# Attention v and q read from PSUM by VectorE, and the blocks of a step laid out anew, in a fused graph layer (gather, attention, routed FFN)

## The reference, cut to what matters

```python
xn = layernorm(x)                                        # 12500 nodes x 256
x  = x + gnn(xn) + mix(xn)[0]
x  = x + ffn(layernorm(x))                               # for the routed half of the nodes

def gnn(x):                                              # 212500 edges
    agg = segment_sum(edge_val[:, None] * x[src], dst)
    return relu(((1 + eps) * x + agg) @ W1.T + b1) @ W2.T + b2

def mix(x):                                              # one node is a sequence of length 1
    h = relu(batchnorm(conv(logmap(x), w_qkv)))          # 768 channels
    t = logmap(proj(expmap(h)))                          # a scale per row
    s = conv(conv(t, w_dw), w_pw)                        # both halves: 1536 channels
    q, k, v = split(scaled(concat(t, s)))                # 16 groups of 32 each
    q, k = relu(q), relu(k)
    out = (v k^T) q / (v + ATT_EPS)                      # = v * q * sum_group(k) / (v + eps)
    ft = logmap(expmap(out)) @ w_res.T + b_res
    return proj(expmap(ft))
```

## Time and profile before

| what | us |
|---|---|
| median of 3 runs | 2632.83 (2632.32 to 2636.76) |
| the profiled execution, its own time | 2637.63 |
| span of that execution | 2636.0 |
| PE busy in the span | 2489.5 (94%), 12654 matmuls |
| DVE busy | 1806.4 (69%) |
| ACT busy | 1464.7 (56%) |
| POOL busy | 1753.3 (67%) |

### The profile page before, as it was taken

The page is one execution under the profiler, slowest core; times in us unless marked ns, Lnnn a source line. Parts: engine busy times, 40 slices in busy tenths (PEclk is TensorE's granted clock), DMA queues, the critical chain, the costliest instruction groups (busy, mean ns, idle before and its releaser), DMA issues.

```text
span 2636.0 us, 42907 instructions
## 1 busy us (share of the span) xinstructions
PE 2489.5 (94%) x12654; PEld 2172.5 (82%) x12654; DVE 1806.4 (69%) x5986; ACT 1464.7 (56%) x3513; POOL 1753.3 (67%) x1858
## 2 busy tenths in 40 slices
PE   5688899999999999999999999999999999999997
PEld 4466688888888888888888888888788888888886
DVE  5754676767767677776776867667676776777657
ACT  4453555655556565565655556556565655656531
POOL 0006777777777777777777777777777777777600
PEclk9798999999999999999999999999999999999998
DMA  7433444344444444434344444443434444343338
GB/s 228 153 115 88 119 118 127 114 121 124 120 125 115 120 124 120 125 116 128 115 121 123 117 126 114 121 123 115 126 115 126 118 121 121 111 129 114 108 116 278
DMA packets 195537, 333.37 MB, mean 126 GB/s; under 512 B 47839, under 2 KB 138013, under 8 KB 195209
## 3 DMA queue, kind: packets, MB, share of 16 engines
q0 software_dynamic: 85216, 233.60, 31.1%
q1 hardware_dynamic: 105018, 92.42, 10.9%
q10 hardware_dynamic: 5072, 4.57, 0.6%
HBM read 291.99 MB, written 38.46 MB: 125 GB/s over the span
## 4 chain that ended last, share of the span: by engine, by line
PE 76%; DVE 9%; ACT 6%; DMA 6%; issue 2%; ACTq 1%; POOL 1%; SPq 0%; DVEq 0%; POOLq 0%
PE bank L1168 23%; PE qkv L1263 13%; PE bank L1275 12%; PE bank L1182 9%; PE bank L1212 6%; PE qkv L1192 4%; DMA work<-in_x 4%; PE qkv L1191 2%; PE bank L1228 2%; PE bank L1237 2%; PE bank L1202 2%; DVE rings L975 2%; DMA rings<-xn_dram,window 1%; DVE work L407 1%; ACT work L465 1%
## 5 line engine op out<-in xcount | busy, mean ns | idle before, releaser
L781 POOL DMA_INDIRECT rings<-xn_dram,window x1764 | 1740.5, 987 | 651.3 <-issue 381.4
L1168 PE MATMUL bank<-rings 128*128 128x256 f32 x3528 | 891.9, 381 | 28.1 <-DMA rings<-xn_dram,window 16.3
L1168 PEld LDWEIGHTS bank<-rings 128*128 128x128 f32 x3528 | 654.6, 190 | 130.2 <-DVE rings L975 32.8
L975 DVE TENSOR_SCALAR rings<-iota,window_dst,window 128x128 f32<-128x128 f32 x1764 | 559.8, 364 | 150.3 <-PE bank L1168 136.2
L1263 PE MATMUL qkv<-work,ffn_weights 128*128 128x256 f32 x1568 | 362.9, 380 | 0.0
L1275 PE MATMUL bank<-ffn_weights,work 128*128 128x256 f32 x1568 | 362.0, 379 | 0.0
L871 ACT ACTIVATE work<-qkv,fb 128x256 f32<-128x256 f32 x392 | 159.6, 472 | 310.5 <-PE qkv L1263 309.9
L1275 PEld LDWEIGHTS bank<-ffn_weights,work 128*128 128x128 f32 x1568 | 297.2, 190 | 40.0
L1263 PEld LDWEIGHTS qkv<-work,ffn_weights 128*128 128x128 f32 x1568 | 293.9, 190 | 37.8
L1182 PE MATMUL bank<-resident,weights 128*128 128x256 f32 x1176 | 279.0, 381 | 0.0
L1182 PEld LDWEIGHTS bank<-resident,weights 128*128 128x128 f32 x1176 | 224.5, 191 | 30.7
(11 more groups left out here) (222 smaller groups left out, 3332.5 us busy)
## 6 DMA issues: line engine op xcount, KB each, us to landing
rings<-xn_dram,window POOLq DMA_INDIRECT x1764, 2.8
xn_dram<-work SPq DMA_DIRECT2D x14, 896.0 KB, 7.7
work<-xn_dram SPq DMA_DIRECT2D x49, 256.0 KB, 3.1
work<-in_x SPq DMA_DIRECT2D x48, 256.0 KB
out<-work SPq DMA_DIRECT2D x48, 256.0 KB
work<-in_x SPq DMA_DIRECT2D x13, 896.0 KB, 5.9
rings<-out SPq DMA_DIRECT2D x6, 896.0 KB, 8.6
out<-rings SPq DMA_DIRECT2D x6, 896.0 KB, 6.8
```

The source lines that it names most:

```text
L781: nc.gpsimd.indirect_dma_start(out=msg[q][:, :], out_offset=None, in_=xn_dram[:, :], in_offset=bass.IndirectOffsetOnAxis(ap=window[t % WIN ...
L975: v.tensor_scalar(sel[k % SEL_RING], iota[:, :], window_dst[b][:, k % SLOTS:k % SLOTS + 1], window[b][:, k % SLOTS, 2:3].bitcast(F32), ALU ...
L1168: te.matmul(agg[h][:, 0:D], sel[k % SEL_RING], msg[q], start=first, stop=last, skip_group_check=True).then_inc(slot_used, 1)
```

## The change: what it does

ScalarE's copy of v (line 815) and its relu of q (line 817) go, and with them the buffer `rq`. VectorE's two instructions of `mix_ratio` now read v and q from PSUM; the relu of q is the max in the second of them, which signals `v_read`. ScalarE's relu of k signals a new semaphore `k_read`, for which `mix_ratio` waits. The minus sign of the formula moves into `mix_recip`. The number of VectorE instructions for a half stays at seven, with one waited link fewer in each half. The two tables are new: on TensorE the second qkv block goes from slot 10 to 11, W2 from 4 to 9, and others by one to three slots; on VectorE `combine` goes from slots 6 and 12 to 8 and 11, `add_b2` from 3 to 4, `ffn_result` from 5 to 2, `mix_n4` from 1 to 2, `mix_f` from 4 to 3, and so on.

```diff
-        rq = view(work, 7936, 512)
...
+        k_read = sem("k_read")
...
-        PE_AT = dict(sup=0, x3=0, qkv=(0, 10), w1=1, h1=(12, 17, 20), w2=4, outT=(13, 23), ft=(16, 27), hid=(23, 23,
-                     27, 29), y=(31, 32, 32, 35))
-        DVE_AT = dict(scale=(5, 10), out=(6, 13), c=(12, 18), ft=(14, 29), sup=(27, 0), n4=1, f=4, y=5, x=3,
-                      combine=(6, 12), rstd=16, tail_out=(20, 24), stage=(0, 27))
...
+        PE_AT = dict(sup=0, x3=0, qkv=(0, 11), w1=1, h1=(13, 18, 20), w2=9, outT=(14, 23), ft=(16, 29), hid=(23, 25,
+                     27, 29), y=(29, 32, 32, 35))
+        DVE_AT = dict(scale=(5, 10), out=(6, 13), c=(12, 19), ft=(15, 31), sup=(23, 0), n4=2, f=3, y=2, x=4,
+                      combine=(8, 11), rstd=16, tail_out=(16, 25), stage=(2, 25))
...
+        def role_in(role):
+            return qkv[:, role].rearrange("p i s c -> p (i s c)")
...
-                q_in, k_in, v_in = (qkv[:, role].rearrange("p i s c -> p (i s c)") for role in range(3))
+                k_in, v_in = role_in(1), role_in(2)
...
-                s.activation(v_raw, v_in, ACT.Copy)
-                s.activation(rk, k_in, ACT.Relu)
-                s.activation(rq, q_in, ACT.Relu).then_inc(v_read, 1)
+                s.activation(rk, k_in, ACT.Relu).then_inc(k_read, 1)
...
-        MIX_LINKS, TAIL_LINKS = 24, 19
+        MIX_LINKS, TAIL_LINKS = 22, 19
...
-                v.tensor_tensor(vs, vs, om, ALU.mult)
+                v.scalar_tensor_tensor(vs, vs, -1.0, om, ALU.mult, ALU.mult)
...
-                dve.wait_ge(v_read, i * 2 + (h + 1))
-                link(v.scalar_tensor_tensor(v_raw, v_raw, s_col[h], om, ALU.mult, ALU.mult))
-                link(v.scalar_tensor_tensor(v_raw, vs, 2.0, v_raw, ALU.subtract, ALU.mult))
+                dve.wait_ge(k_read, i * 2 + (h + 1))
+                link(v.scalar_tensor_tensor(v_raw, role_in(2), s_col[h], om, ALU.mult, ALU.mult))
+                v.scalar_tensor_tensor(v_raw, role_in(0), 0.0, v_raw, ALU.max, ALU.mult).then_inc(v_read, 1)
...
-                link(v.scalar_tensor_tensor(om, rq, -1.0, v_raw, ALU.mult, ALU.mult))
+                dve.wait_ge(v_read, i * 2 + (h + 1))
+                link(v.scalar_tensor_tensor(om, vs, 2.0, v_raw, ALU.add, ALU.mult))
```

## The result

The changed kernel takes **2659.7 us** (median of 4 runs, 2657.63 to 2663.57) against 2633.18 us (4 runs, 2632.32 to 2636.76): ratio 1.010, 95% interval 1.0082 to 1.0117. It is 1.0% slower. The forecast was 2649, with a range of 2635 to 2662.

The account below looks back on a forecast made before the run. TensorE, busy 2138 of 2180 us, was taken as the bound. Steps with FFN +21.8 and without -6.4 sum to +15.4 us, giving 2653.0 from the profiled time or 2648.2 from the median; forecast 2649, range 2635 to 2662.

Parts of the forecast that it names:

- the F step: Main-loop step with FFN: 48.21 us, 0.52 above the present mean; 42 such steps add 21.8 us.
- the loop began 3.9 us earlier: First stage, ahead of the main loop: taken as unchanged, bounds 2 us either way.
- The wait at the second qkv block: TensorE arrives at 11.07 us, waits 0.83 us every step for VectorE's v_read and starts at 11.90; about 40 us in all.
- A PSUM operand costs nothing: VectorE's two mix_ratio instructions: zero price for reading PSUM, bounds a gain of 0.02 and a loss of 0.05 us a pair.
- the signal: Semaphore from VectorE's v_read to TensorE's second qkv block: 0.05 us added.
- tail_out at 16 and 25: VectorE's slot table: costs nothing, as VectorE has 650 us of slack and its selection matrices are 8 slots ahead.
- Steps without FFN: Main loop: mix_c's 1.16 us wait goes, 37.45 us against a mean of 38.73; five steps give -6.4 us.
- The worse rival: ScalarE's mix_n4 waits for ft(0), delaying the second om's copy; half a us late would be +21 us, 2670; chance 0.13.
- GpSimd's gathers take 1661 of 2180 us with 18 buffers, not the bound: Main loop: GpSimd's gathers, busy 1661 of 2180 us, were counted among what costs nothing.
- the faster rival: VectorE chain from line 814 to v_read ends 0.83 us earlier: 2615 from the profiled time, 2610 from the median; chance 0.09.
- v_read isn't late: Claim of the faster rival: v_read comes in time, steps with FFN at 47.40 and without at 36.6 us; chance 0.09.

Follow-up runs that it names:

- The variants without that wait: Two runs: the kernel before with the new slot tables, 2660.3 us; the changed kernel with VectorE forming relu(q) * v early, 2644.06 us.
- slots alone: The kernel before, its formula kept, with the new tables of slots: 2660.3 us, ratio 1.0094; on the first group's chip 3105.5 us.
- third group: Chip where before takes 3027.47 us; with 4 of 36 gathers omitted: before 2857.73, changed 2959.27, slots alone 2965.03 us; product early, one wait per three gathers, 3089.29.
- first group: Chip where before takes 3044.7 us: changed kernel with old tables 3026.85, slots alone 3105.5, changed with tail_out at 20 3071.1, with product early 3096.87 us.

## Why the prediction was right, and where it wasn't

The forecast added +15.4 us, the spans differ by 22.9, the medians of the runs by 26.5. The place and the cause of the wait were right. The sum was too small mostly in one term, the F step, by 35 x 0.30 = 10.5 us; against that the loop began 3.9 us earlier, which the forecast had bounded at 2.

- **The wait at the second qkv block**: right in place, line and size (0.82 us for 0.83; 37.2 us in all for "about 40"). The end of line 996 came at 11.91 for 11.85. From there to TensorE took 0.14 us, where I had 0.05.
- **A PSUM operand costs nothing**: right. The two instructions that read PSUM take 745 and 692 ns; before, from SBUF, they took 744 and 692 (lines views, the changed kernel and then before):

```profile
L995 DVE SCALAR_TENSOR_TENSOR work<-qkv,work 128x512 f32<-128x512 f32 x98 | 73.0, 745 | 0.0
L996 DVE SCALAR_TENSOR_TENSOR work<-qkv,work 128x512 f32<-128x512 f32 x98 | 67.8, 692 | 3.3
...
L994 DVE SCALAR_TENSOR_TENSOR work<-work 128x512 f32<-128x512 f32 x98 | 72.9, 744 | 0.0
L995 DVE SCALAR_TENSOR_TENSOR work<-work 128x512 f32<-128x512 f32 x98 | 67.8, 692 | 3.3
```

Each has one input in PSUM and the other in SBUF. The Trainium skill's 58 against 120 cycles (VectorE: DVE Perf Modes, the section on the TRN2 errata), which would make two instructions 0.13 us longer, is not borne out by these rows.
- **The F step, +0.52 us**: too small, +0.82. About 0.1 is the signal. Another 0.24 is an edit listed among those that cost nothing, "tail_out at 16 and 25". In the steps from 1963 to 2252 the changed kernel takes 48.28 us, in the others 48.5, and what differs is a weight load that waits for the selection matrix of slot 25, behind rstd and tail_out(0). It is 31 of the 58 waits in the row of 38.2 us above, 0.37 us each. That tail_out makes it late is read from the timeline; the run with tail_out at 20 was on the chip where before takes 3044.7 and can't show it, as the changed kernel has no time there. So for this part of the term the cause is argued, not shown.
- **Steps without FFN**: 37.37 us for 37.45, right.
- **The worse rival** (mix_n4 behind ft(0)) didn't come: nothing holds the second om's copy, and the projection behind it waits for that copy once, 0.8 us.
- **"GpSimd's gathers take 1661 of 2180 us with 18 buffers, not the bound"**: this is the step that failed. It read the busy share and left out the 0.30 us gap that stands behind every gather. With it, 1685 gathers x 1.291 us fill 2175 of the 2180 us, and the kernel before was within 2.2 us a period of this bound. The failure cost the forecast itself next to nothing, since TensorE waits only 1.5 us for gathers in the changed kernel's loop; it made the faster rival (2615 us) look possible.

**What the time hangs on.** The forecast's mechanism is the true one for the changed kernel in this sense: its period is TensorE's, 425.7 us, 1.1 over what the gathers need. But it isn't worth what the forecast says. A "v_read isn't late" would not have given 2615 us. The variants without that wait, 2660.3 and 2644.06 us, run at the pace of their gathers (periods of 425.1 for 424.7 and 422.6 for 422.4), and they wait for gathers in the step behind the one without FFN. That the two agree, with not one gap over 0.35 us and with TensorE's 16.3 and 20.5 us of waits for gathers, is measured. That fewer or cheaper gathers would free these variants on this chip was not shown.

**Why the gathers got slower.** In each of three traces (before, after, slots alone) I put every gather between 300 and 2480 us beside VectorE's instructions. Gathers with no VectorE work beside them take 0.95 us in all three: the gather itself hasn't changed. Over 1.15 us are 166, 197 and 177 of them, and each of these has a VectorE instruction that starts 0.15 to 0.7 us after it. That alone says little, as three gathers in four have one (1233 of 1664 in the changed kernel); the lines say more. In the changed kernel these are, for the most part, line 1002 (63 gathers, of 63 with that line there) and line 990 (60 of 62), both 512 wide with both inputs in SBUF, and the selection matrices. The timeline of GpSimd and VectorE in the changed kernel shows one long and one short:

```profile
1415.59 0.94 POOL L781 DMA_INDIRECT rings<-xn_dram,window  x1 [0.30 <-issue]
...
1416.76 0.68 DVE L1001 SCALAR_TENSOR_TENSOR work<-work 128x512 f32<-128x512 f32 x1
1416.83 1.43 POOL L781 DMA_INDIRECT rings<-xn_dram,window  x1 [0.30 <-issue]
1417.48 0.69 DVE L1002 TENSOR_TENSOR work<-work 128x512 f32<-128x512 f32 x1
```

Line 1002 starts 0.65 us into the gather, and the gather takes 1.43 us for 0.94. VectorE can pay too: tail_out's multiply takes 529 ns in place of 408 on average, 590 where it starts 0.15 to 0.7 us into a gather and 403 elsewhere. The Trainium skill (SBUF — State Buffer, the section "Who interferes with whom") says that a VectorE instruction with two SBUF inputs contends with a GpSimd instruction that reads SBUF, and that the order of issue decides which of them is blocked. Lines 1002 and 990 agree with the first half: every long gather with one of them ends 0.09 us after that instruction does. With the second half they don't agree as recorded: the gather began first, and it is the gather that got longer, while the VectorE instruction kept its 0.69 us.

Of the same window, 0.15 to 0.7 us, three more lines tell something:

- Line 996 of the changed kernel, with q in PSUM: 64 gathers, none long. The instruction in its place before (line 995, both inputs in SBUF): 40 of 67 long, and 46 of 46 with the new slots alone. Reading from PSUM seems to spare the gathers, so the arithmetic of the change is not what slowed them.
- Lines 999 of before and 1001 of the changed kernel, 512 wide with both inputs in SBUF: 67 and 29 gathers, none long. So two SBUF inputs are not enough by themselves.
- The tensor_reduce, with one input: 17 of 19 long before (line 998), none of 63 in the changed kernel (line 999).

Neighbouring instructions start in the same half microsecond, so no count parts one line from the next for certain. As far as they go, it is where VectorE's 512-wide instructions fall against the gathers that sets GpSimd's pace, and a new table of slots shifts that. This was read from timelines and not tried by an edit.

**What stays open.** Whether the new table costs the kernel something beside the gathers' pace; whether a table exists that keeps the gathers at 0.95 us, which on GpSimd's side would be 324 x (1.006 - 0.946) = 19 us a period; what tail_out at slot 16 costs on the chip of the result; and the arithmetic with the old table on the chip of the result.

## What to carry to other kernels

An engine's busy share is not its load. Multiply the count of its repeated instruction by start-to-start time, and look whether it ever truly waits for anyone: an engine at 67% that never does is the bound, or close to it. Then look at whether the others wait for it: in the changed kernel they didn't (1.5 us), in two variants they did (16.3 and 20.5 us). Where two engines are that close, a wait taken from the one gains little unless the load of the other falls too. And where GpSimd issues many small gathers, count their mean duration again after every move of VectorE's wide SBUF instructions.

## What the runs showed of the hardware

- A gather of 128 rows costs GpSimd 0.95 us and 0.30 us before the next, with or without a wait on the semaphore ahead of it (median gap 0.305 us in every trace).
- Beside some 512-wide VectorE instructions with both inputs in SBUF a gather takes up to 0.5 us longer (0.94 to 1.43 us, lines 990 and 1002), beside others it doesn't (line 1001), and beside the one that reads q from PSUM it doesn't either (line 996).
- A scalar_tensor_tensor 512 wide takes the same time with one of its inputs in PSUM as with both in SBUF (745 and 692 ns for 744 and 692).
- Chips differ more than the change does: before takes 2633 us on two occasions and 3027 and 3045 us on two others. There most instructions take as long as ever (a gather 0.98 to 1.00 us, the norm 1.45 us), but ScalarE often starts 4 to 6 us after the record of its releaser has ended. No record shows what it waits for. On the chip of the third group the new slots suffer more from it than the old (5.4 us a step for 0.04); on that of the first group the old slots with the new arithmetic have it too (2.6 us). TensorE's granted clock is below 1.00 in the main loop there, 0.92 to 0.98, and its residual matmuls, which wait for ScalarE there, take 513 ns on average with the slots alone (first group) in place of 381.
